# Gelu written twice by ScalarE, without a rounding copy, in a fused attention and feed-forward kernel

## The reference

```
xn  = layernorm(x)
out = x + attn(xn) + ffn(xn)

attn: q, k, v = xn @ W + b, 16 heads of 16;  q = elu(q) + 1;  k = elu(k) + 1
      k = k / sqrt(sum(k * k) + 1e-6)           # per row and head
      o = q @ (k^T @ v)  (no softmax);  y = xn + o @ Wo + bo
      (y - mu) / sqrt(var + 1e-6) * gamma + beta
ffn:  h = xn
      three times:  g = gelu(layernorm(qlora(h, W[2j])) * lng[j] + lnb[j])   # erf form
                    h = qlora(g, W[2j+1]) + h
qlora: 4-bit codes, scaled by group of 16, plus a rank-32 product and a bias
```

## Time and profile before

| | |
|---|---|
| median of 3 runs | 621.18 us (621.06 to 621.93) |
| profiled execution | 621.54 us, its span 619.8 us |
| busy: TensorE, VectorE, ScalarE, POOL | 587.2, 495.2, 446.1, 372.9 us |
| granted TensorE clock, mean | 0.998 of full speed |
| Gelu passes / rounding copies | 96 / 96 |

### The profile page before, as it was taken

How to read it: one execution, slowest core, us unless ns; L and a number is a source line. 1 busy time by engine, 2 the same in 40 slices (tenths; PEclk the granted TensorE clock), 3 DMA queues, 4 the chain that set the end, 5 groups by cost and what they waited for, 6 DMA issues and landing times.

```text
span 619.8 us, 10199 instructions
## 1 busy us (share of the span) xinstructions
PE 587.2 (95%) x3285; PEld 499.4 (81%) x3285; DVE 495.2 (80%) x1084; ACT 446.1 (72%) x699; POOL 372.9 (60%) x361
## 2 busy tenths in 40 slices
PE   4999999999998999989999999989999899999995
PEld 4787889778896889868798788968889687986885
DVE  3678789787888869797797868978697987977587
ACT  3577777859768588686787687785886957967752
POOL 4656645577454956467554684548655585646555
PEclk9999999999999999999999999999999999999999
DMA  9003000500032000500004000240004100030001
GB/s 272 29 2 136 1 0 35 171 1 1 1 119 85 0 0 0 187 16 0 0 34 169 0 0 0 79 124 0 0 0 163 40 0 0 25 111 2 0 2 69
DMA packets 11460, 29.01 MB, mean 47 GB/s; under 512 B 2592, under 2 KB 4272, under 8 KB 11440
## 3 DMA queue, kind: packets, MB, share of 16 engines
q1 hardware_dynamic: 10960, 28.35, 13.5%
q10 hardware_dynamic: 480, 0.41, 0.3%
HBM read 20.37 MB, written 8.39 MB: 46 GB/s over the span
## 4 chain that ended last, share of the span: by engine, by line
PE 65%; ACT 21%; DVE 6%; issue 5%; POOL 2%; DMA 1%; ACTq 0%; DVEq 0%; POOLq 0%
PE bank L1469 16%; PE bank L1596 9%; PE bank L1475 8%; PE bank L1640 6%; PE bank L1585 5%; ACT fw L630 5%; PE bank L1542 4%; PE bank L1561 3%; ACT L663 3%; ACT gh L635 3%; PE bank L1569 2%; PE bank L1552 2%; ACT hTh L639 2%; PE bank L1529 2%; PE bank L1462 2%
## 5 line engine op out<-in xcount | busy, mean ns | idle before, releaser
L262 POOL TENSOR_TENSOR gl<-fw,gh 128x512 fp32r<-128x512 f32 x80 | 103.9, 1310 | 63.1 <-ACT gh L635 62.9
L417 POOL TENSOR_TENSOR sqs<-fw 128x512 f32<-128x512 f32 x48 | 63.4, 1321 | 86.6 <-ACT fw L620 85.6
L620 ACT ACTIVATE fw<-bank,b1c 128x512 f32<-128x512 f32 x96 | 61.8, 685 | 61.0 <-PE bank L1475 61.0
L630 ACT ACTIVATE fw<-fw,vec 128x512 f32<-128x512 f32 x96 | 75.4, 808 | 7.9 <-DVE fw L953 6.8
L953 DVE SCALAR_TENSOR_TENSOR fw<-bank,b1c,rb 128x512 f32<-128x512 f32 x96 | 68.3, 745 | 10.0 <-ACT rb L626 9.9
L392 POOL TENSOR_TENSOR rsf<-vef,neghalf 128x4 f32<-128x4 f32 x48 | 52.2, 1087 | 31.1 <-DVE vef L944 29.6
L267 POOL TENSOR_TENSOR hTl<-hT,hTh 128x512 fp32r<-128x512 f32 x40 | 52.1, 1320 | 18.4 <-ACT hTh L639 18.0
L1596 PE MATMUL bank<-K,XN 128*128 128x256 f32 x256 | 62.0, 380 | 0.0
L392 POOL TENSOR_TENSOR rs<-ve,neghalf 128x2 f32<-128x2 f32 (+1 forms) x48 | 41.3, 860 | 33.6 <-DVE ve L1041 29.5
L1640 PE MATMUL bank<-M,qT 128*128 128x256 f32 x256 | 59.4, 379 | 0.0
L635 ACT ACTIVATE gh<-fw 128x512 fp32r<-128x512 f32 x96 | 56.9, 621 | 0.8
(11 more groups left out here) (155 smaller groups left out, 1573.0 us busy)
## 6 DMA issues: line engine op xcount, KB each, us to landing
X<-in_L_attn_x_dram SPq DMA_DIRECT2D x16, 512.0 KB, 5.8
RES<-in_L_attn_x_dram SPq DMA_DIRECT2D x16, 512.0 KB, 4.4
out_dram<-RES SPq DMA_DIRECT2D x14, 512.0 KB, 2.7
XNB<-in_L_ffn_qweights_dram SPq DMA_DIRECT2D x2, 512.0 KB, 8.2
out_dram<-RES SPq DMA_DIRECT2D x4, 256.0 KB, 2.3
RES<-in_L_ffn_qweights_dram SPq DMA_DIRECT2D x1, 512.0 KB, 9.7
Y<-in_L_ffn_lora_a_dram ACTq DMA_DIRECT2D x4, 96.0 KB, 6.5
Wp<-in_L_attn_Wk_dram SPq DMA_DIRECT2D x1, 256.0 KB, 5.9
```

Source lines behind the costliest of these rows:

```text
L262: engine.tensor_tensor(gl[:, h, m, :], fw[:, h, m, :], gh[:, h, m, :].bitcast(F32), ALU.subtract).then_inc(g_low[h][m], 1)
L417: pool.tensor_tensor(sqs[:, h, :], fw[:, h, 0, :], fw[:, h, 1, :], ALU.add).then_inc(sqs_ready[h], 1)
L620: act.activation(fw[:, h, m, :], FB[h][m][:], ACT.Square, bias=b1c[:, m, j:j + 1]).then_inc(sq_ready[h], 1)
L630: act.activation(fw[:, h, m, :], fw[:, h, m, :], ACT.Gelu, bias=lnb[:, m, j:j + 1], scale=lng[:, m, j:j + 1]).then_inc(g_ready[h], 1)
```

## The change

ScalarE now computes each Gelu twice from the same normalised input: g_rounded writes it straight into the rounded tile gh, and g_whole writes it in float32 in place in fw. The copy is gone. g_rounded carries the wait for the normalised input, g_whole has none. g_lower waits for g_whole (g_ready) in place of gh (g_high); the two passes of a tile are always issued in the order rounded, whole. second_high still waits for gh alone.

```diff
         def g_lower(engine, i, h, j, m):
-            engine.wait_ge(g_high[h], nth(i, NBLK * NC, j * NC + m))
+            engine.wait_ge(g_ready[h], nth(i, NBLK * NC, j * NC + m))
...
-            def gelu(i, h, j, m):
+            def g_rounded(i, h, j, m):
                 act.wait_ge(yn_ready[h], nth(i, NBLK * NC, j * NC + m))
+                act.activation(gh[:, h, m, :], fw[:, h, m, :], ACT.Gelu, bias=lnb[:, m, j:j + 1],
+                               scale=lng[:, m, j:j + 1]).then_inc(g_high[h], 1)
+
+            def g_whole(i, h, j, m):
                 act.activation(fw[:, h, m, :], fw[:, h, m, :], ACT.Gelu, bias=lnb[:, m, j:j + 1],
                                scale=lng[:, m, j:j + 1]).then_inc(g_ready[h], 1)
-
-            def g_higher(i, h, j, m):
-                act.wait_ge(g_ready[h], nth(i, NBLK * NC, j * NC + m))
-                act.activation(gh[:, h, m, :], fw[:, h, m, :], ACT.Copy).then_inc(g_high[h], 1)
```

All lists of all engines are new orders of the same calls (with the two Gelu calls in place of the old two). No other call is added or removed. The parts of body(i) that matter below, first ScalarE:

```diff
                 k_exp(i, 3, BODY)
-                gelu(i, 0, 0, 0)
+                g_rounded(i, 0, 0, 0)
                 k_square(i, 3)
                 rb_copy(i, 1, 0, BODY)
-                g_higher(i, 0, 0, 0)
-                gelu(i, 1, 0, 0)
-                gelu(i, 0, 0, 1)
-                g_higher(i, 0, 0, 1)
-                gelu(i, 1, 0, 1)
+                g_whole(i, 0, 0, 0)
+                g_rounded(i, 0, 0, 1)
+                g_rounded(i, 1, 0, 0)
+                g_whole(i, 1, 0, 0)
+                g_rounded(i, 1, 0, 1)
+                g_whole(i, 1, 0, 1)
+                g_whole(i, 0, 0, 1)
                 q_exp(i, 0, 0, BODY)
-                g_higher(i, 1, 0, 0)
-                g_higher(i, 1, 0, 1)
-                q_exp(i, 0, 1, BODY)
                 h_higher(i, 0, 0, 0)
                 h_higher(i, 0, 0, 1)
-                q_exp(i, 1, 0, BODY)
...
-                gelu(i, 0, 1, 0)
+                g_rounded(i, 0, 1, 0)
+                g_whole(i, 0, 1, 0)
+                g_rounded(i, 0, 1, 1)
                 rb_copy(i, 1, 1, BODY)
+                g_whole(i, 0, 1, 1)
                 g_copy(i)
-                gelu(i, 0, 1, 1)
-                g_higher(i, 0, 1, 0)
-                g_higher(i, 0, 1, 1)
-                gelu(i, 1, 1, 0)
-                gelu(i, 1, 1, 1)
-                g_higher(i, 1, 1, 0)
-                g_higher(i, 1, 1, 1)
-                ln1_normalise(i + 1, 0, BODY)
+                g_rounded(i, 1, 1, 0)
+                g_rounded(i, 1, 1, 1)
+                g_whole(i, 1, 1, 0)
+                g_whole(i, 1, 1, 1)
+                q_exp(i, 1, 1, BODY)
                 h_higher(i, 0, 1, 0)
                 h_higher(i, 0, 1, 1)
-                q_exp(i, 1, 1, BODY)
+                ln1_normalise(i + 1, 0, BODY)
+                h_higher(i, 1, 1, 0)
                 m_copy(i, BODY)
-                h_higher(i, 1, 1, 0)
                 h_higher(i, 1, 1, 1)
```

TensorE, body(i): second_high of both halves now goes before second_low of either in block 0, and in the middle:

```diff
                 second_high(i, 0, 0, BODY)
+                second_high(i, 1, 0, BODY)
                 second_low(i, 0, 0)
-                second_high(i, 1, 0, BODY)
                 second_low(i, 1, 0)
...
                 turn_squares(i, 1, 1, BODY)
+                spread_rstd(i, 0, 1, BODY)
                 add_g(i, 3, BODY)
-                spread_rstd(i, 0, 1, BODY)
+                project_q(i, 1, 1, BODY)
                 add_g(i, 4, BODY)
                 add_g(i, 5, BODY)
+                spread_rstd(i, 1, 1, BODY)
                 add_g(i, 6, BODY)
-                spread_rstd(i, 1, 1, BODY)
                 add_g(i, 7, BODY)
-                project_q(i, 1, 1, BODY)
+                second_high(i, 0, 1, BODY)
                 make_vk(i, BODY)
-                second_high(i, 0, 1, BODY)
                 second_low(i, 0, 1)
```

In head() the two halves' products of block 0 also change places:

```diff
-                second_high(0, 0, 0, HEAD)
-                second_low(0, 0, 0)
                 second_high(0, 1, 0, HEAD)
+                second_high(0, 0, 0, HEAD)
+                second_low(0, 0, 0)
+                project_q(0, 1, 0, HEAD)
                 second_low(0, 1, 0)
```

More of the change, by code:

```diff
@@ L502, in body @@
                 ffn_root(i, 1, 0)
+                base_xn(i, 1, BODY)
                 g_lower(pool, i, 0, 0, 0)
@@ L523, in body @@
                 add_squares(i, 0, 2)
+                base_xn(i, 3, BODY)
                 ln2_root(i, 0)
@@ L554, in tail @@
                 g_lower(pool, i, 0, 1, 1)
+                base_xn(i, 2, TAIL)
                 g_lower(pool, i, 1, 1, 0)
@@ L557, in tail @@
                 h_lower(pool, i, 0, 1, 1)
-                base_xn(i, 2, TAIL)
                 add_squares(i, 0, 2)
+                base_xn(i, 3, TAIL)
                 ln2_root(i, 0)
@@ L812, in body @@
                 square(i, 0, 1, 1, BODY)
+                q_exp(i, 0, 1, BODY)
+                q_exp(i, 1, 0, BODY)
                 square(i, 1, 1, 0, BODY)
@@ L835, in body @@
                 xt_copy(i + 1, 0, 0, BODY)
+                ln1_normalise(i + 1, 1, BODY)
                 square(i, 1, 2, 0, BODY)
@@ L880, in tail @@
                 h_higher(i, 1, 0, 1)
-                q_exp(i, 0, 1, TAIL)
                 square(i, 0, 1, 0, TAIL)
+                square(i, 0, 1, 1, TAIL)
                 q_exp(i, 1, 0, TAIL)
-                square(i, 0, 1, 1, TAIL)
                 square(i, 1, 1, 0, TAIL)
@@ L1754, in head @@
                 first_high(0, 0, 0, HEAD)
+                first_low(0, 0, 0)
                 row_sums()
-                first_low(0, 0, 0)
                 xt(0, 1, 0, None)
@@ L1781, in head @@
                 first_low(0, 0, 1)
-                project_q(0, 1, 0, HEAD)
                 first_high(0, 1, 1, HEAD)
+                first_low(0, 1, 1)
+                add_g(0, 0, HEAD)
                 turn_squares(0, 0, 1, HEAD)
+                add_g(0, 1, HEAD)
+                add_g(0, 2, HEAD)
+                turn_squares(0, 1, 1, HEAD)
                 shift_sums()
-                add_g(0, 0, HEAD)
-                first_low(0, 1, 1)
-                add_g(0, 1, HEAD)
                 spread_rstd(0, 0, 1, HEAD)
-                add_g(0, 2, HEAD)
                 add_g(0, 3, HEAD)
-                turn_squares(0, 1, 1, HEAD)
                 add_g(0, 4, HEAD)
                 add_g(0, 5, HEAD)
+                spread_rstd(0, 1, 1, HEAD)
                 add_g(0, 6, HEAD)
-                spread_rstd(0, 1, 1, HEAD)
+                project_q(0, 1, 1, HEAD)
+                add_g(0, 7, HEAD)
                 second_high(0, 0, 1, HEAD)
-                add_g(0, 7, HEAD)
-                project_q(0, 1, 1, HEAD)
-                make_vk(0, HEAD)
                 second_low(0, 0, 1)
@@ L1803, in head @@
                 second_low(0, 1, 1)
+                make_vk(0, HEAD)
+                first_high(0, 0, 2, HEAD)
                 make_m(0, HEAD)
-                first_high(0, 0, 2, HEAD)
                 first_low(0, 0, 2)
@@ L1845, in body @@
                 turn_squares(i, 1, 0, BODY)
+                project_q(i, 0, 0, BODY)
+                spread_rstd(i, 1, 0, BODY)
                 project_q(i, 0, 1, BODY)
[L1847 to L1848 removed]
                 project_q(i, 1, 0, BODY)
                 second_high(i, 0, 0, BODY)
+                second_high(i, 1, 0, BODY)
                 second_low(i, 0, 0)
[L1852 removed]
                 second_low(i, 1, 0)
@@ L1918, in tail @@
                 project_q(i, 0, 1, TAIL)
-                project_q(i, 0, 0, TAIL)
+                project_q(i, 1, 0, TAIL)
                 spread_rstd(i, 1, 0, TAIL)
@@ L1922, in tail @@
                 second_low(i, 0, 0)
-                project_q(i, 1, 0, TAIL)
+                project_q(i, 0, 0, TAIL)
                 second_high(i, 1, 0, TAIL)
@@ L1930, in tail @@
                 first_low(i, 1, 1)
+                turn_squares(i, 0, 1, TAIL)
                 add_g(i, 1, TAIL)
-                turn_squares(i, 0, 1, TAIL)
                 add_g(i, 2, TAIL)
```

377 lines of the change are left out of this document (186 added, 191 removed), and 14 rows, old and new, of tables (BODY_USES, HEAD_USES, TAIL_USES).

## The result

The changed kernel takes 626.12 us (median of four runs, 623.91 to 627.32), the kernel before 621.12 beside it (four runs, 620.77 to 621.93). By the medians it is 5.0 us slower, by the means 4.6. The ratio is 1.0074 (95% interval 1.0045 to 1.0104), close to that of the means. So it is slower by 0.7%, or 625.8 us against the 621.18 shown, 0.2 inside the upper end of the forecast range. The profiled execution (623.91, span 622.1) is the shortest of the four, so it shows 2.4 of the 5.0 us; the other three spans, 624.1 to 625.5, are 2.0 to 3.4 us longer.

The account below looks back on a forecast made before the run. TensorE's own work was taken as the bound (busy 70.6 of 73.0 us per loop batch). First batch -1.2, six loop batches +1.8 and last batch +0.1 gave +0.7; forecast 621.7 us, range 616.0 to 626.0.

Parts of the forecast that it names:

- The load order: First batch: Wq and half of x come later by some 256 KB, neither due for 2 us or more.
- The last batch: Final batch: late gl, a turn and a spread later, a wait shrinking by 0.7, end not moving; +0.1 us.
- the port: Rival, loop: VectorE's gl 11 meets POOL on the shared port, 1.1 us more each, 630 us; chance 0.05.
- The first batch: The wait of 1.18 us goes, 0.55 of waiting for gl returns, a further 0.2 gained; -1.2 us.
- Block 0 of the loop: The 1.18 us wait for gh goes, late gl brings waits of 0.4 and 0.8; 0.2 of 1.33 us left.
- The wait at spread_rstd(0,1): Middle of a loop batch: new TensorE wait of 0.2 us, since the spread can start 4.6 us after first_low.
- Second half: Loop batch: g_copy at 291.2, 10.0 us to the squares at 301.1 to 301.2, turn_squares(0,2) 0.3 us late.
- the term of +1.8: Six loop batches, each +0.3 us from turn_squares(0,2) coming late.
- Prices: ScalarE: Gelu into the rounded tile 808 ns, both kinds 155 us busy; table loads 1.28 us, unchanged in number.
- The slower outcome: Two rivals: ScalarE as the bound, 0.26, 625.4 us, and the port, 0.05, 630 us; together chance 0.31.
- ScalarE as the bound: Rival, loop between g_copy and the squares: g_copy later than 291.2, 0.6 us a batch, 625.4 us; chance 0.26.
- My prediction's rule: SBUF ports: a VectorE instruction with two SBUF inputs and a POOL instruction take turns, each for its whole length.

Follow-up runs that it names:

- e9: Kernel before, with one load moved: Wk ahead of the second half of x; 624.00 us, ratio 1.0035.
- e2: Kernel before, with SyncE's first loads in the changed kernel's order and nothing else; 624.02 us, ratio 1.0035.
- e1: Changed kernel, with SyncE's first loads in the order of the kernel before; 623.64 us, ratio 1.0030.
- e5: e4 with TensorE's first calls in the old order, three keep_busy in one piece ahead of bias_mean; 621.85 us, ratio 0.9999.
- e4: e1 with VectorE's ffn_var of half 1 back behind the second ffn_normalise in the last batch, block 2; 622.58 us, ratio 1.0009.
- e8: e5 with three keep_busy ahead of vec_transpose and four more added in two pairs; 620.06 us, ratio 0.9978.
- e12: Kernel before, with TensorE's first calls as in e8 and nothing else; 620.78 us, ratio 0.9986.
- e10: e8 with codes 0, lora_b and the scales loaded ahead of Wk and Wq; as run, six keep_busy ahead of vec_transpose; 625.20 us, ratio 1.0063.
- e11: Changed kernel with its own load order, and TensorE's first calls as in e8; 624.04 us, ratio 1.0039.
- e3: Kernel before with the Gelu written twice, old orders except two whole passes of block 0 moved ahead of q_exp; 629.71 us, ratio 1.0128.
- e6: e5 with the loop's whole Gelu pass 01 of block 0 moved directly behind its rounded pass; 624.19 us, ratio 1.0051.
- e7: e6 with VectorE subtracting gl 11 of block 0 ahead of residual 00 in the loop; 625.73 us, ratio 1.0070.

## Why the prediction was right or wrong

The forecast was 621.7, most likely no change; the result is 5.0 us slower. That it lies within the range, by 0.2 us, is luck: the upper end was set by mechanisms of the loop that did not come. By its own steps:

- **The load order.** This is the step that failed: "the changed load order makes Wq and half of x later by some 256 KB, and neither is due for 2 us or more". It was costed at nothing by asking only which loads come later in SyncE's list. The load that TensorE waits for first is on ScalarE's queue, 1 to 6 KB each, and shares the way with SyncE's: it came 1.95 us later in the profiled run (e9: 2.2 from Wk alone), and e2 puts the order by itself at 2.5 us. That the order moves this wait is shown both ways; why the short loads are held up is not.
- **The new first calls of TensorE and VectorE**, not costed at all. e1 still loses 1.9 us between the first wait and qk_sums (11.02 against 9.14): the later fast pace and the shift calls that meet POOL. bias_mean's place is worth 0.7 (e5 against e4). Counted by medians from the kernel before beside each, the 5.0 come down to 2.1 with the old loads (e1), 1.1 with the old end (e4), 0.4 with bias_mean back (e5) and -1.4 with the early start (e8), which the kernel before can have too (-1.0, e12). For the three longer runs of the changed kernel themselves there is no trace, so how the two share their 2.0 to 3.4 us was not shown.
- **The last batch**, forecast +0.1, measured +1.13. The end "does not move" was argued from TensorE's rows and the order of finish; the port was weighed as a rival for the loop only. e4 shows it at 1.0.
- **The first batch**, forecast -1.2: measured -0.84 from the first weight transpose to turn_squares(0,2). Right in kind; e12 and e8 bear it out.
- **Block 0 of the loop.** Right, somewhat mis-sized. The wait of 1.18 went, waits for gl came at the two places named: the first inside second_low (four matmuls in 1.44 in place of 1.10), the second with 0.54. From the first rounded Gelu to first_high(0,1) it is 10.79 in place of 11.17, so 0.38 of 1.33 stay, forecast 0.2.
- **The wait at spread_rstd(0,1).** Forecast 0.2, measured 0.24 (285.25, 0.68 behind the turn in place of 0.44).
- **Second half.** Forecast squares at 301.1 to 301.2 and turn_squares(0,2) 0.3 late. From g_copy to the squares it took 9.93, forecast 10.0, but g_copy came 0.4 sooner than walked, so the squares were in time and the turn too. The loop batch is 73.03, forecast 73.3, before 73.06: the term of +1.8 measured +0.25. It is 0.4 lost at the entry to the loop, where no step of the sum looked, less 0.03 in each batch behind it.
- **Prices.** The Gelu into the rounded tile takes 808 ns, as taken; the two kinds 151.6 us busy, forecast 155; table loads unchanged at 1283 ns.

The slower outcome had 0.31, but for other mechanisms: ScalarE as the bound did not come; the port did, at the end and, in e1, e4, e10 and e11, in the first stretch, neither of them the place that I had named. In the loop of the changed kernel it lengthens one instruction (1.39 us at 271.93), behind which VectorE waits for TensorE anyway; in e3, e6 and e7 TensorE waits for it.

## What to carry to other kernels

Two small VectorE instructions between SBUF tiles can cost more than a Gelu pass if POOL runs beside them; so before an order is changed, lay POOL's long instructions against VectorE's chains of short ones, and count an idle POOL there as worth something. The order of the first loads is not free even for loads that are due late: look at what the first engine waits for, on whichever queue it is, and let no warm-up work depend on a load. When a change rewrites everything, the start and the end need their own line in the sum; here the loop, which the argument was about, moved by 0.03 us a batch.

## What was not expected of the hardware

- VectorE instructions with one SBUF input are held by POOL as well: the CAST of 2 elements at 1.05 us in place of 0.16, and it ended as POOL's multiplication did (17.52 and 17.50). My prediction's rule spoke of two inputs. The same section of the Trainium skill (SBUF — State Buffer, SBUF: two separate sides) also names VectorE instructions in a 2-port mode beside those with two inputs; that this CAST runs in it is not shown here.
- A chain of dependent short instructions can be met twice in a row: of 0.29 us each, two cost 2.55 (e6) while POOL's three subtractions follow each other from 265.97 to 270.09.
- The fast pace of TensorE came at a moment that differs between runs: 24 matmuls of L1648 took 5.05 us in the kernel before and 5.3 in e5; with the same calls and the same start at 3.46 they took 4.4 in e8, 5.2 in e11 and 5.3 in e12, at a granted clock of 1.00 in every row. e8's early start made it harmless, and the range of the runs fell from 2.4 us (e5) to 0.5.
- A stop of 1.60 us behind 5 us of work was followed by a granted clock of 0.50 from 12 to 14 us (e11), one of 2.03 us behind 14 us of nearly unbroken work by none below 1.00 (e10).
